# Expert rows of a mixture of experts added by indirect DMAs onto a copy of x2 in DRAM, in a fused GNN and MoE kernel

## The reference

```python
x = x + gnn(layernorm(x))        # per node: sum, max, mean of its edges; concat with x and u; MLP 608 -> 1024 -> 256; + its input
x2 = layernorm(x)                # below, x is the x1 of the kernel
logits = x2 @ gate_w + gate_b
vals, idx = top_k(logits, 2); w = softmax(vals)
moe = w[0] * expert[idx[0]](x2) + w[1] * expert[idx[1]](x2)   # expert: relu(x2 @ w1 + b1) @ w2 + b2, 256 -> 512 -> 256
y = x2 + moe
return x + layernorm(y) * gamma + beta
```

## Time and profile before

| | us |
|---|---|
| median of three timed runs | 1554.78 (1553.64 to 1555.97) |
| the run of the profiled execution | 1560.4 |
| its span, first to last instruction | 1558.7 |
| its mean granted TensorE clock | 0.867 of 2.4 GHz |

### The profile page before, as it was taken

How to read it: one execution, slowest core, us unless ns; L and a number is a source line. 1 busy time by engine, 2 the same in 40 slices (tenths; PEclk the granted TensorE clock), 3 DMA queues, 4 the chain that set the end, 5 groups by cost and what they waited for, 6 DMA issues and landing times. The chain is left out here.

```text
span 1558.7 us, 27971 instructions
## 1 busy us (share of the span) xinstructions
PE 1143.0 (73%) x6527; PEld 1031.4 (66%) x6528; DVE 864.4 (55%) x2995; ACT 622.1 (40%) x1869; POOL 766.6 (49%) x953
## 2 busy tenths in 40 slices
PE   2009989899999999999982669999999999300000
PEld 1008878788887888888871569999999999300000
DVE  6978997997998990000007934343443434155445
ACT  5854645555555556565630013323232323111111
POOL 4776656565666666767520023323333333377760
PEclk6558999999999999999995889999999999755555
DMA  9876587676767565111109022222222222345553
GB/s 300 275 247 250 181 315 252 234 255 244 274 242 250 191 235 162 49 39 50 32 26 321 15 88 74 67 73 68 70 71 67 74 67 72 109 129 171 170 159 109
DMA packets 123776, 236.86 MB, mean 152 GB/s; under 512 B 29629, under 2 KB 94036, under 8 KB 123596
## 3 DMA queue, kind: packets, MB, share of 16 engines
q1 hardware_dynamic: 70997, 175.31, 31.0%
q0 software_dynamic: 33424, 41.57, 10.2%
q10 hardware_dynamic: 19303, 19.50, 4.2%
HBM read 122.34 MB, written 113.64 MB: 151 GB/s over the span
## 5 line engine op out<-in xcount | busy, mean ns | idle before, releaser
L888 PE MATMUL ps<-mem 96*128 96x250 f32 x1200 | 291.2, 378 | 0.0
L827 ACT ACTIVATE mem<-ps,mem 128x128 f32<-128x128 f32 x452 | 129.3, 369 | 371.1 <-PE ps L974 371.1
L888 PEld LDWEIGHTS ps<-mem 96*128 96x128 f32 x1200 | 231.2, 193 | 27.8
L886 PE MATMUL ps<-mem 128*128 128x250 f32 x800 | 209.8, 385 | 24.8 <-ACT mem L724 23.4
L974 PEld LDWEIGHTS ps<-mem 128*128 128x128 f32 x1808 | 221.8, 193 | 7.4 <-DVE mem L1204 1.7
L974 PE MATMUL ps<-mem 128*128 128x128 f32 x1808 | 222.4, 276 | 1.3 <-DVE mem L1204 1.3
L982 PE MATMUL ps<-mem 128*128 x904 | 213.7, 379 | 0.0
L1042 DVE TENSOR_TENSOR_SCAN mem<-ps,mem 128x80 f32<-128x80 f32 x960 | 207.9, 301 | 0.3
L1046 DVE TENSOR_TENSOR_SCAN mem<-ps,mem 128x80 f32<-128x80 f32 x960 | 207.8, 304 | 0.0
L886 PEld LDWEIGHTS ps<-mem 128*128 128x128 f32 x800 | 151.7, 193 | 47.2 <-ACT mem L724 28.0
L898 PE MATMUL ps<-mem 128*125 128x256 f32 x800 | 181.6, 379 | 0.6 <-ACT mem L724 0.6
(11 more groups left out here) (190 smaller groups left out, 1522.5 us busy)
## 6 DMA issues: line engine op xcount, KB each, us to landing
run_sum<-mem SPq DMA_DIRECT2D x40, 960.0 KB
run_max<-mem SPq DMA_DIRECT2D x40, 960.0 KB
mem<-in_edge_attr_dram SPq DMA_DIRECT2D x36, 960.0 KB
mem<-in_L_ffn_w_dram SPq DMA_DIRECT2D x32, 512.0 KB
expert_rows<-mem SPq DMA_DIRECT2D x113, 128.0 KB, 1.9
mem<-in_x_dram ACTq DMA_DIRECT2D x25, 250.0 KB
x_plus_beta<-mem ACTq DMA_DIRECT2D x25, 250.0 KB
x_normed<-mem ACTq DMA_DIRECT2D x25, 250.0 KB
```

The costliest lines, as they stand in the source:

```text
L827: ins = act.activation(hT[b][:, c, :], bank(2 + b, c * P, (c + 1) * P), ACT.Relu, bias=eb1c[:, bass.ds(e, 1), c])
L886: pe.matmul(h, W1x[:, c, hc * P:(hc + 1) * P], XT[b][:, c, :], start=(c == 0), stop=False)
L888: ins = pe.matmul(h, W1a[:, s, hc * P:(hc + 1) * P], AT[b][:, s, :], start=False, stop=(s == 2))
```

## The change

The sum of x2 and the two weighted expert rows is no longer gathered at the end. It is built up in DRAM while the experts run.

- **GNN.** ScalarE stores x2 twice: into `x2_d`, whose rows now have two more columns for the weights (258 floats), and into the first 6250 rows of `ya_d`. It stores x1 itself from `GO`, in the middle of the next step (`store_x1`), and not x1 + beta. `X1B` and its add on GpSimd are gone; `take_g` waits for the store of x1 before it overwrites `GO`. Rows lie in DRAM so that the two rows of a partition are neighbours (`by_pair`).
- **Routing.** The weights are worked out earlier, and SP writes them into the last two columns of `x2_d` by two DMAs with runs of 8 bytes. The table of slots now holds a code: which node, and whether it is its first or second expert. Six short VectorE operations make of it the rows to gather (`fromU`), the rows to add to (`intoU`; empty slots go to rows of their own behind row 8192) and a mark (`second`).
- **Experts.** VectorE picks each row's weight out of the gathered columns (128x1) and multiplies `YO` by it. GpSimd adds `YO` onto the rows `intoU` of `ya_d` by an indirect DMA with `compute_op=ALU.add`. Since the rows of two tiles can be the same, each waits until the one before has landed. GpSimd's loop: gather of tile i+4, index copy for the gather of tile i+5, adding DMA of tile i, index copy for the adding DMA of tile i+1. SP stores nothing here.
- **Last stage.** 14 batches of one or two macros. SP loads x1 (four batches are issued before the expert loop's end, beside it) and the finished sums from `ya_d`, four batches ahead; VectorE takes the statistics, ScalarE normalises, GpSimd adds beta to x1 and multiplies by gamma, VectorE adds both, SP stores.

The core of the diff:

```diff
-    x2_d = nc.dram_tensor("x2_normed", [N, D], F32).ap()
-    x1b_d = nc.dram_tensor("x1_plus_beta", [N, D], F32).ap()
-    ys_d = nc.dram_tensor("expert_rows", [SLOT_TILES * P, D], F32).ap()
+    x2_d = nc.dram_tensor("x2_and_weights", [N, D + 2], F32).ap()
+    x1_d = nc.dram_tensor("x1_rows", [N, D], F32).ap()
+    ya_d = nc.dram_tensor("x2_plus_experts", [KEYS + SLOT_TILES * P, D], F32).ap()
...
+            sp.wait_ge(weights_ready, 1)
+            for a in range(2):
+                sp.dma_start(batch_rows(x2_d, 0, MACROS)[:, :, a, D:D + 2], wsel[:, a::2, :], allow_slow_non_contiguous=True).then_inc(weights_stored, 16)
             sp.wait_ge(dve_free, 1)
...
-            def store_y(i, g, b):
-                sp.wait_ge(y_ready, i + 3)
-                sp.dma_start(ys_d[bass.ds(i * P, P)], YO[b]).then_inc(yo_stored[b], 16)
-            in_pairs(sp, SLOT_TILES, store_y)
...
+            for n in range(DEEP):
+                load_x1(n)
+            sp.wait_ge(yo_stored[0], (SLOT_TILES - SLOT_TILES // 2) * 16)
+            sp.wait_ge(yo_stored[1], SLOT_TILES // 2 * 16)
+            for n in range(DEEP):
+                load_y(n)
+            for n, (m0, m1) in enumerate(BATCHES):
+                if n + DEEP < len(BATCHES):
+                    sp.wait_ge(f_norm, n + 1)
+                    load_y(n + DEEP)
+                    sp.wait_ge(f_beta, n + 1)
+                    load_x1(n + DEEP)
+                sp.wait_ge(f_out, n + 1)
+                sp.dma_start(out[m0 * M:m1 * M].rearrange("(a p) d -> p a d", p=NT), FO[n % 2][:, 0:2 * (m1 - m0)]).then_inc(out_stored[n % 2], 16)
...
-                pool.wait_ge(x1_ready, i + 1)
-                pool.wait_ge(x1b_stored, (i + 1) * 16)
-                pool.tensor_tensor(X1B, GO, betabc, ALU.add).then_inc(x1b_ready, 1)
...
             def slot_rows(i, g, b):
-                hold(pool, xt_psum, i + 1)
-                pool.tensor_copy(slot_now[b], slotU[:, bass.ds(i, 1)]).then_inc(slot_copied, 1)
+                hold(pool, xt_ready, i + 1)
                 hold(pool, slot_copied, i + 1)
...
             def expert_rows(i, g, b):
-                hold(pool, er_read, i + 1)
...
+                hold(pool, y_ready, i + 3)
+                hold(pool, into_copied, i + 1)
+                if not isinstance(i, int) or i >= 2:
+                    hold(pool, yo_stored[1 - b], (g + b) * 16)
+                elif i == 1:
+                    hold(pool, yo_stored[0], 16)
+                pool.indirect_dma_start(out=ya_d, out_offset=bass.IndirectOffsetOnAxis(into_now[b], 0), in_=YO[b], in_offset=None,
+                                        compute_op=ALU.add).then_inc(yo_stored[b], 16)
+
+            def slots_step(i, g, b):
+                if not isinstance(i, int) or i + 4 < SLOT_TILES:
+                    slot_rows(*after(i, g, b, 4))
+                if not isinstance(i, int) or i + 5 < SLOT_TILES:
+                    next_from(*after(i, g, b, 5))
+                expert_rows(i, g, b)
+                if not isinstance(i, int) or i + 1 < SLOT_TILES:
+                    next_into(*after(i, g, b))
...
+                act.dma_start(by_pair(x2_d)[bass.ds(MACROS - 1 - i, 1), :, :, 0:D], X2now).then_inc(x2_st, 16)
+                act.dma_start(by_pair(ya_d[0:N])[bass.ds(MACROS - 1 - i, 1)], X2now).then_inc(y_begun, 16)
...
             def take_slots(i, g, b):
+                dve.wait_ge(xg_got[b], (g + 1) * 16)
+                dve.scalar_tensor_tensor(out=slotw[:, bass.ds(i, 1)], in0=XG[b][:, D + 1:D + 2], scalar=second[:, bass.ds(i, 1)], in1=XG[b][:, D:D + 1],
+                                         op0=ALU.mult, op1=ALU.add).then_inc(slot_weighed, 1)
...
-                dve.wait_ge(yo_stored[b], (g + 1) * 16)
-                dve.tensor_tensor(YO[b], bank(6 + b, 0, D), eb2bc[:, bass.ds(e, 1), :].rearrange("p o d -> p (o d)"), ALU.add).then_inc(y_ready, 1)
+                if not isinstance(i, int) or i >= 2:
+                    dve.wait_ge(yo_stored[b], g * 16)
+                dve.tensor_tensor(YO[b], bank(6 + b, 0, D), eb2bc[:, bass.ds(e, 1), :].rearrange("p o d -> p (o d)"), ALU.add).then_inc(y_added, 1)
+                dve.wait_ge(slot_weighed, i + 3)
+                hold(dve, y_added, i + 1)
+                dve.tensor_scalar(YO[b], YO[b], slotw[:, bass.ds(i, 1)], None, ALU.mult).then_inc(y_ready, 1)
```

More of the change, by code:

```diff
@@ L164, in gnn_moe_kernel @@
         gammabc = k.take(D, parts=NT)
-        betabc = k.take(2, D, parts=NT)
+        betabc = k.take(D, parts=NT)
         gwt = k.take(DC, NX)
@@ L266, in gnn_moe_kernel @@
         a = Area(mem, KEPT, ROUTE_END)
-        XG = [a.take(D) for _ in range(2)]
+        XG = [a.take(D + 2) for _ in range(2)]
         XgT = [a.take(DC, P) for _ in range(2)]
@@ L328, in gnn_moe_kernel @@
         yo_stored = [sem(f"expert_rows_stored{i}") for i in range(2)]
[L329 to L334, removed]
+        fx_got = [sem(f"final_x1_got{i}") for i in range(DEEP)]
+        fy_got = [sem(f"final_y_got{i}") for i in range(DEEP)]
+        f_step, f_var, f_sd, f_stat, f_norm, f_scaled, f_beta, f_out = (sem(f"final_{n}") for n in ("step", "var", "sd", "stat", "norm", "scaled", "beta", "out"))
         out_stored = [sem(f"out_stored{i}") for i in range(2)]
@@ L373, in _ @@
             weight(b2bc, spread(row(gb2, NT), 1, 2))
-            weight(betabc, spread(row(beta, NT), 1, 2))
+            weight(betabc, row(beta, NT))
             weight(gwt, gate_w.rearrange("(c p) e -> p c e", p=P))
@@ new lines, in slots_step @@
+            def slots_step(i, g, b):
[6 more added lines that the diff above has]
+                    next_into(*after(i, g, b))
+            next_from(0, 0, 0)
+            for i in range(4):
+                slot_rows(i, i // 2, i % 2)
+                next_from(*after(i, i // 2, i % 2))
@@ new lines, in _, with add_beta @@
+            next_into(0, 0, 0)
+            slots_step(0, 0, 0)
+            slots_step(1, 0, 1)
+            in_pairs(pool, SLOT_TILES, slots_step, ahead=5, first=2)
+            def add_beta(n):
+                a = 2 * (BATCHES[n][1] - BATCHES[n][0])
+                pool.wait_ge(fx_got[n % DEEP], (n // DEEP + 1) * 16)
+                if n >= 2:
+                    pool.wait_ge(f_out, n - 1)
+                pool.tensor_tensor(FB[n % 2][:, 0:a], FX1[n % DEEP][:, 0:a], spread(betabc, 1, a), ALU.add).then_inc(f_beta, 1)
@@ L782, in gnn_step @@
                         carry_in(*after(i, g, b))
+                    if norm and hc == 4:
+                        store_x1(i - 1)
                     if norm and hc in (4, 5):
@@ L1263, in _, with moments @@
-            combine(0, 0, 0)
-            in_pairs(dve, TILES // CB, combine_step, ahead=1)
+            expert_step(0, 0, 0)
+            expert_step(1, 0, 1)
+            in_pairs(dve, SLOT_TILES, expert_step, ahead=2, first=2)
+            def moments(n):
+                b, tiles = n % 2, 2 * (BATCHES[n][1] - BATCHES[n][0])
+                dve.wait_ge(fy_got[n % DEEP], (n // DEEP + 1) * 16)
+                for a in range(tiles):
+                    f1.mark(dve.bn_stats(statc[b][:, a, :], FY[n % DEEP][:, a, :]))
+                f1.wait()
+                for a in range(tiles):
+                    f1.mark(dve.bn_aggr(mvc[b][:, a, :], statc[b][:, a, :]))
+                f1.wait()
+                dve.sem_inc(f_var, 1)
@@ L1268 @@
+            f1 = Steps(dve, f_step)
+            moments(0)
+            for n in range(len(BATCHES)):
+                scale_shift(n)
+                if n + 1 < len(BATCHES):
+                    moments(n + 1)
+                finish(n)
 _INS = ['x', 'dst', 'edge_attr_96', 'L0_gnn_u', 'L0_gnn_W1', 'L0_gnn_b1', 'L0_gnn_W2', 'L0_gnn_b2', 'L0_ffn_gate_w',
```

253 lines of the change are left out of this document (126 added, 127 removed).

## The result

The changed kernel takes 1606.15 us (median of 4 runs, 1601.74 to 1615.07) where the kernel before takes 1554.41 us: ratio 1.0339, 95% interval 1.0292 to 1.0386. It is 52 us slower. The forecast was 1515 us, 40 us faster, with a range that ended at 1600 us. The profiled execution is the slowest of the four, 1613.4 us of span against 1558.7 us before.

What follows compares the result with a forecast made beforehand. The prediction took few DMA engines, shared by plain and indirect transfers, to bound the last stage; 1558.7 - 64 + 28 - 5 + 1 = 1519 us of span, 1515 us as median run, own range 1495 to 1550, 8-in-10 range 1478 to 1600.

Steps and rivals of the forecast that it cites:

- What bounds the kernel: Last stage, 219.7 us: plain transfers (159 us) and indirect loads (49 us) share a few DMA engines that bound it, 208 us.
- Part 1: Last stage: without the 100 indirect loads, 144 us of transfers at 121 GB/s; end at 1495 instead of 1558.7 us, -64 us.
- The allowance for gaps: Last stage: 5 us allowed for gaps in the queue of transfers; 5 us less without gaps.
- Ahead of the queue: Before the last stage's transfers: last tile's bias add, scaling and adding DMA, about 4.3 us after TensorE's end.
- Part 2: Expert loop: the chain of adding DMAs, each waiting for the last to land, lengthens the period from 3.73 to 3.98 us, +28 us.
- The bounds, 2.2 and 6.4 us: Expert loop, adding DMA's chain: 2.2 us from a plain store plus issue gap, 6.4 us from the slowest gather landing plus waiting.
- (b): Expert loop: chain or GpSimd's own work becomes the bound and eats the gain from 4.33 us on; 1597 us, chance 0.2.
- (a): Expert loop: adding DMA lands within 2.9 us of issue, chain hides, period stays 3.73 us; 1487 us, chance 0.2.
- (c): Expert loop: VectorE's copy blocks GpSimd's issue, 0.70 us per tile, period 4.68 us; 1594 us, chance 0.1.
- (d): Last stage doesn't shorten: each of 14 batches waits for its own load, arithmetic and store; 1579 us, chance 0.05.
- Part 3: GNN: GpSimd's beta add and its store wait go, ScalarE waits for x1's store, one more store per macro; -5 us, bounds -13 and +8.
- Part 4: Routing: two more short operations, at most +1 us; the weights' two transfers of 3125 8-byte runs are free, +0.

## Why the prediction was wrong, point by point

**What bounds the kernel: right.** The reading of the last stage, few engines shared by plain and indirect DMAs, was tested in three kernels: cut by partitions, the stage falls from 144 to 82 us and from 217 to 190 us, and with 30 MB it takes 247 us where 250 were worked out. The Trainium skill's page "DMA: Bandwidth & Descriptors" says in "Why a DMA increments its semaphore by 16 and not by 1" that a DMA runs on the largest number of engines up to 16 that divides the slowest dimension on both of its sides: 5 for 125 rows, 16 for 112. The shares of three and nine tenths agree with it.

**Part 1, the last stage: right, with a piece of luck.** Forecast were 152 us from the first load's issue, 144 of them transfer; it took 144.4 us in all, its 17.4 MB at 117 to 129 GB/s in the full slices. The allowance for gaps was not needed: the DMAs ran at 3 tenths without a pause until the last 6 us. Ahead of the queue the forecast was short: 4.3 us from TensorE's last product to the last landing, and 14.5 us measured, since the slow chain of part 2 had three adding DMAs still to issue. The two errors cancel in the sign that the prediction named, 150 to 160 us from TensorE's last product to the end: it was 158.8 us.

**Part 2, the expert loop: the step that failed.** The mechanism was named, with its place (GpSimd's wait for the DMA before), its condition and the period from which it decides, 4.33 us; its size was taken at 3.98 us and is 4.85. The term "the gather of the same 128 rows, 2.8 us, plus the second read of 128 KB, 0.35 us" came to 3.15 us and measured 3.9. All of the difference lies in the issue, which takes 1.71 us with an addition and in which I had left the gather's 0.97. Behind the issue 2.2 us were forecast (2.8 - 0.97 + 0.35) and 2.2 measured (3.9 - 1.71), but by luck: a plain indirect write needs 1.4 us there (2.4 - 1.0) and not the gather's 1.8, and the addition puts 0.8 us on top and not 0.35. The bounds, 2.2 and 6.4 us, held the value. But between ends so far apart I took the middle row and gave it a range of half a microsecond, where each 0.1 us counts 11 us of run time. The last term, landing to next issue, was near: 0.83 forecast, 0.86 in the usual period and 0.89 on the mean. Two of the prediction's own signs of being wrong came: adding DMAs further apart than 4.33 us, and an issue far over 1 us. (4.85 - 3.98) x 113 = 98 us; the forecast's span of 1519 and the measured 1613.4 are 94 apart, as the tail of the chain (some 10 us) and the quicker last stage nearly cancel.

**The rivals.** (b) is what happened, with chance 0.2. Its price was worked out by GpSimd's own work, 4.7 us, which gave 1597 us: near the number for a wrong reason, since that work hides below 3.77 us with the wait gone. The gaps between GpSimd's instructions are about 0.17 us there where I had 0.34 to 0.83. (a), 1487 us, is what both the kernel without the wait (1489.5) and the one without the addition (1491.3) show. (c), VectorE's copy, exists but is worth 0.12 to 0.16 us per tile, not 0.70. The rule of the Trainium skill's page "SBUF — State Buffer", section "SBUF: two separate sides", on which it hung is borne out in kind, by the issue's 1707 ns with the copy and 1607 without. What (c) made of it was too much: in the changed kernel the 102 issues that met the copy ran beside it for 0.57 us on the mean and were 0.15 us longer. Why they lose so little is not shown. (d) fell: the batches overlap.

**Part 3, the GNN: right in sign.** The wait at L535 is gone, and TensorE's wait there for ScalarE is 15.8 us instead of the 23.4 of the earlier trace rows. The last product of the GNN's second layer started at 810.7 and 806.1 us in the two profiles with the old GNN and at 797.9 to 803.9 us in the nine with the new one, and the first gather of the expert stage, behind the routing, at 906.7 and 901.8 against 892.7 to 900.7 us. The ranges don't meet, but the two old ones alone lie 5 us apart, so the size is uncertain. No experiment undid this part alone.

**Part 4, the routing: right.** The two DMAs with runs of 8 bytes moved their 6250 runs between about 856 and 869 us, some 2 ns per run and neither nothing nor 8.5 ns. They were done 30 us ahead of the last slot number at 899 us, and nothing waited for them.

**The sum.** Right: -64 forecast and -73 measured for the last stage (with the start of its loads counted in), -4 and -5 ahead of the loop. Wrong: +28 against +132 for the loop. The chance of "slower", 0.32, was too low for a term that no row showed and whose bounds reached to both sides of the threshold.

## What to carry to other kernels

Before DMAs are put in a chain where each waits for the landing of the last, work out the period from landing plus the way back to the next issue, set it against the loop's own period, and if no row shows the operation, treat the answer as open: here 0.6 us decided between a gain and a loss. Often the chain can be taken out of the data: two tables in which no two tiles add onto the same row needed no order between tiles, kept the addition in DRAM and took 96 us off. And look at the number of partitions of plain DMAs: 125 rows ran at a third of the engines, and cutting each into 112 and 13 gave 24 us in one kernel and 66 in the other, with nothing else changed.

## What the runs showed of the hardware

- An adding indirect DMA of 128 rows of 1 KB onto DRAM: 1.57 to 2.12 us of issue, 3.9 us from issue to landing; the plain one, 1.00 and 2.4 us; the adding one of 64 rows, 1.44 and 3.1 us.
- An adding DMA takes three times the share of the DMA engines and three times the packets of a plain one with the same bytes: 31.7 against 10.5 points and some 11,470 against 3820 packets in 300 us.
- The way from its landing to the issue of the next one that waits for it: 0.86 us in the usual period.
- An adding DMA's issue that met VectorE's copy of 128x1024 took 1.74 to 1.99 us on the mean, one that did not 1.60.
- Plain DMAs over 125 partitions: 117 to 129 GB/s with rows of 1 to 2 KB, share 0.3; over 112 and 13 partitions mostly 200 to 330 GB/s, at nine tenths.
- VectorE's addition of two tiles of 125x1024 took 1.23 us alone and 2.98 us beside GpSimd's passes over such tiles. The Trainium skill's page "SBUF — State Buffer", section "Who interferes with whom", says that a VectorE operation with two inputs in on-chip memory and a GpSimd operation that reads there shut each other out; the two times agree with it.
